# Where the output-gate fold, the quantum columns and half of the modulation loads stand in an adaLN retention layer

## The chip, the cores and the metric

The kernel runs on the 8 cores of one Trainium2 chip. Each core computes one element of the batch, with the whole layer on it; the cores exchange nothing. The metric is the device time in microseconds (us) of the slowest core.

## What is computed

For each of 8 batch elements (2048 rows of 1024), with a modulation vector from a small matrix product:

```python
mod = (silu(c) @ wmod).reshape(B, 6, 1, -1)            # c: 8 x 1024, wmod: 1024 x 6144
sa, ca, ga, sb, cb, gb = (mod[:, k] for k in range(6))
ga, gb = clamp away from zero: sign(g) * max(|g|, 0.25)
h = layernorm(x) * (1 + ca) + sa
x = x + ga * ((silu(h @ W_G) * groupnorm(retention(h @ Wq, h @ Wk, h @ Wv))) @ W_O)
h = layernorm(x) * (1 + cb) + sb
x = x + gb * (relu(quantum(h @ W1 + b1)) @ W2 + b2)
# quantum(z) = z + 0.1 * (cos(th) * wr + sin(th) * wi) * wi * sin(th + 0.1 * z), th, wr, wi: 4096 values
```

Retention has 8 heads of 128 columns and a causal decay of its own per head.

## The kernel before

The program has three blocks, each ended by a barrier of all engines: the prologue (`blk_p`), phase A with the retention (`blk_a`), and phase B with the feed-forward part (`blk_b`). Helpers of the class `Prog` record operations in program order, one list per engine; a block's list is issued by its engine strictly in that order, and waits on semaphores are put in where a tile was written or read by another engine. `dma_in` puts a load on SyncE's queue and lets four be in flight, `dma_cast` puts one on GpSimd's queue (two in flight; it may change the type), `dma_out` one on ScalarE's.

The prologue loads constants, makes `silu_cols` and four sets of 32 columns (`b1_cols`, `th_cols`, `wr_cols`, `wi_cols`), and calls `emit_matvec_half(0)` (L429 is its matmul). The matrix-vector product with `wmod` has two halves of 3072 output columns. For each of 8 blocks of rows `dk` and 4 parts it loads a piece of 128 x 768 f32 (384 KB) to one of two slots of `wmp` and does 6 matmuls of one column into bank 6 of PSUM; after the four parts VectorE adds the 24 columns to `macc` (L440). The third of the parts thus needs the slot of the first. After the call in program order come the casts of X tiles 0 and 1, of the four weights wq, wk, wv and wg (8 pieces each) and of X tiles 2 to 15: 48 in all, each read as 512 KB of f32 and landed as 256 KB of bf16 (L176 is the helper's line). Then `clamp_cols` and `cols_to_tile` make `ga_tile` from half 0; 16 multiplications (L532) fold `ga_tile` into W_O as `wo_bf`, each with a 256 KB load to one of two slots of `wstage`; and some 75 small operations of VectorE and four Sin of ScalarE (L540 to L588) make the quantum columns `p_cols` and `r_cols`, which are read first in phase B.

Phase A goes over 8 groups of 256 rows. Group g issues `stage_W(g-2)` (output projection with `wo_bf`, from L897), `stage_R(g-1)` (retention, from L738), `stage_Pmm(g)` (the four projections; `wg` ends it), `stage_Pstats(g+1)` (layer-norm statistics, its last operation writes `hpre`, L623) and, for g up to 5, one or two rows of blocks of `emit_matvec_half(1)`: `mod_pieces` gives row 0 to group 0 and rows 1 and 2 to group 1. Phase B keeps both large weights in memory that phase A's tiles had, so it loads them (L176, 64 casts) behind the barrier, and goes over 8 groups of rows again.

Of the kernel before, what the change touches and what calls it, by code (L numbers as in the profile page):

```python
# [255 lines left out]
def _emit(nc, usage, debug, upto="B"):  # L256
# [15 lines left out]
    wm_h = nc.dram_tensor("L0_wmod", [D, 6 * D], F32, kind="ExternalInput").ap()  # L272
# [5 lines left out]
    dbg_h = {}  # L278
# [11 lines left out]
    with ExitStack() as ctx:  # L290
        P = Prog(nc, ctx, usage)

        def alloc(c_, name, pdim, fdim, dtype=F32):
            return c_.enter_context(nc.sbuf_tensor(name, [pdim, fdim], dtype))
# [22 lines left out]
        ab_ctx = ctx.enter_context(ExitStack())  # L317
# [101 lines left out]
        def emit_matvec_half(half, dks=range(8)):  # L419
            for dk in dks:  # L420
                for part in range(4):
                    s = (dk * 4 + part) % 2
                    c0h = half * 3072 + part * 768
                    P.dma_in(wmp[:, s * 768:(s + 1) * 768],
                             wm_h[dk * 128:(dk + 1) * 128, c0h:c0h + 768],
                             writes=[("wmp", s)])
                    for c in range(6):
                        ci = part * 6 + c
                        P.op("tensor", lambda e, s=s, c=c, ci=ci, dk=dk: e.matmul(  # L429
                                psum[6][:, ci:ci + 1],  # L430
                                wmp[:, s * 768 + c * 128:s * 768 + (c + 1) * 128],
                                silu_cols[:, dk:dk + 1],
                                start=True, stop=True),
                             reads=[("wmp", s), "silu_cols"], writes=[("pb", 6)])
                mk = ("macc", half)
                if dk == 0:
                    t_copy("vector", macc[:, half * 24:half * 24 + 24],
                           psum[6][:, 0:24], [("pb", 6)], [mk])
                else:
                    P.op("vector", lambda e, half=half: e.tensor_add(  # L440
                            macc[:, half * 24:half * 24 + 24],
                            macc[:, half * 24:half * 24 + 24], psum[6][:, 0:24]),
                         reads=[("pb", 6), mk], writes=[mk])

        def emit_mod_right_final():
# [7 lines left out]
                 reads=["gb_cols", "b2_cols"], writes=["ctmp2"])  # L453
            cols_to_tile(ctmp2, "ctmp2", gbb2_tile, "gbb2_tile")

        with ExitStack() as pctx:
            cstage = alloc(pctx, "cstage", 8, 128)
            b2stage = alloc(pctx, "b2stage", 8, 128)
            vstage = alloc(pctx, "vstage", 32, 4 * 128)
            th_cols = alloc(pctx, "th_cols", 128, 32)  # L460
            wr_cols = alloc(pctx, "wr_cols", 128, 32)
            wi_cols = alloc(pctx, "wi_cols", 128, 32)
            beta_cols = alloc(pctx, "beta_cols", 128, 32)
            tmpc = alloc(pctx, "tmpc", 128, 32)
            tmpc2 = alloc(pctx, "tmpc2", 128, 32)
            sth_cols = alloc(pctx, "sth_cols", 128, 32)
            cth_cols = alloc(pctx, "cth_cols", 128, 32)
            a_cols = alloc(pctx, "a_cols", 128, 32)

            for name, dst in [("ones_row", ones_row), ("mask4_t", mask4_t),  # L470
                              ("id_bf", id_bf), ("id_f32", id_f32),
# [51 lines left out]
            clamp_cols(ga_cols, "ga_cols", 16)  # L523
            cols_to_tile(ga_cols, "ga_cols", ga_tile, "ga_tile")

            for dk in range(8):
                for hf in range(2):
                    stg = (dk * 2 + hf) % 2
                    P.dma_in(wstage[:, stg * 512:(stg + 1) * 512],
                             Wo_h[dk * 128:(dk + 1) * 128, hf * 512:(hf + 1) * 512],  # L530
                             writes=[("wstg", stg)])
                    P.op("vector", lambda e, dk=dk, stg=stg, hf=hf: e.tensor_mul(  # L532
                            wbf["wo"][:, dk * 1024 + hf * 512:dk * 1024 + (hf + 1) * 512],
                            wstage[:, stg * 512:(stg + 1) * 512],
                            ga_tile[:, hf * 512:(hf + 1) * 512]),
                         reads=[("wstg", stg), "ga_tile"], writes=[("wo", dk, hf)])

            def reduce_range(key, buf):
                for _ in range(8):
                    P.op("vector", lambda e: e.tensor_scalar(  # L540
# [50 lines left out]
            if debug:  # L591
                P.dma_out(dbg_h["d_pcols"], p_cols[:, :], reads=["p_cols"])
                P.dma_out(dbg_h["d_rcols"], r_cols[:, :], reads=["r_cols"])
                P.dma_out(dbg_h["d_ga"], ga_tile[:, :], reads=["ga_tile"])

            if upto == "P":
                P.final_join()
            with nc.Block("blk_p") as blk:
                P.flush(blk)
            if upto == "P":  # L600
                return P.usage

        with ExitStack() as actx:

# [332 lines left out]
            for g in range(NG):  # L937
                if g >= 2:
                    stage_W(g - 2)
                if g >= 1:  # L940
                    stage_R(g - 1)
                stage_Pmm(g)
                if g + 1 < NG:
                    stage_Pstats(g + 1)
                if g in mod_pieces:
                    emit_matvec_half(1, dks=mod_pieces[g])
            stage_W(NG - 2)
# [213 lines left out]
```

## Time and profile before

| | us |
|---|---|
| median of 2 runs | 2183.44 |
| lowest, highest | 2179.59, 2187.28 |
| device time of the profiled execution | 2194.06 |
| span of its slowest core (core 7), from first to last instruction | 2192.5 |
| spans of its eight cores | 2170.7 to 2192.5 |

The profile is one execution, on its slowest core. PE is TensorE's matmuls, PEld its weight loads, DVE VectorE, ACT ScalarE, POOL GpSimd, SP SyncE; a q behind an engine's name means its queue of DMAs and semaphores. L numbers are lines of the kernel before. PEclk is TensorE's granted clock, as a share of full speed. Times in the trace count from the span's start. The views that are read are the page's engine rows and slices, a table of busy time by stretch, lists of instructions in order of time (idle time before an instruction, and what ended it, stand in brackets), one line's instructions and the DMA answers of a stretch.

### The profile page before, as it was taken

The page shows a single profiled execution, that of the slowest core. Times are in us where ns is not written, and L with a number is a line of the kernel's source. Part 1 is how long each engine was busy: PE and PEld are TensorE (multiplying, and loading weights), DVE is VectorE, ACT ScalarE, POOL GpSimd, SP SyncE. Part 2 cuts the span into 40 slices and gives each one's busy share as a digit, 9 for nine tenths or more (in the row PEclk, how much of TensorE's full clock was granted, in tenths as well). Part 3 has the DMA queues.
Part 4 walks back from the last instruction along what each step waited for, and adds up shares of the span by engine and source line. Part 5 has one row for each costly group of instructions (what it writes and reads, how often), then busy time and mean ns, then how long its engine had stood idle before and what let it go on. Part 6 is the DMA issues. An engine that isn't in the chain of part 4 may idle for free.

```text
span 2192.5 us, 23636 instructions; the slowest of 8 cores (2170.7 to 2192.5 us)
## 1 busy us (share of the span) xinstructions
PE 1186.4 (54%) x6720; PEld 733.7 (33%) x6720; DVE 747.0 (34%) x1759; ACT 573.9 (26%) x1255; POOL 93.4 (4%) x132
## 2 busy tenths in 40 slices
PE   3553358484848575473503323474747474756564
PEld 3552236252534353241101111242424242423232
DVE  0002532434353434434301111434353435353433
ACT  0000032122122212222001111343434343434343
POOL 1110000000000000000011110000000000000000
PEclk9999967676867776776556666796969797979888
DMA  7882011010001010000143442000000000000000
GB/s 148 163 163 91 15 29 37 22 30 1 30 1 30 1 44 1 1 1 1 17 65 58 63 62 43 20 1 20 1 20 1 20 1 20 1 20 1 10 11 20
DMA packets 33616, 70.12 MB, mean 32 GB/s; under 512 B 4161, under 2 KB 4434, under 8 KB 33490
## 3 DMA queue, kind: packets, MB, share of 16 engines
q0 software_dynamic: 16128, 29.37, 9.3%
q1 hardware_dynamic: 12754, 30.85, 4.7%
q10 hardware_dynamic: 4608, 8.39, 1.0%
q8 instruction: 58, 0.95, 0.2%
q14 instruction: 68, 0.56, 0.1%
HBM read 89.56 MB, written 8.39 MB: 45 GB/s over the span
## 4 chain that ended last, share of the span: by engine, by line
DVE 15%; ACT 11%; DMA 11%; issue 9%; PE 2%; ACTq 1%; DVEq 1%; POOL 0%; POOLq 0%
DMA w2bf<-L_ffn_W 6%; ACT csin L1051 5%; DMA w1bf<-L_ffn_W 5%; DVE t1b L1065 5%; DVE t1b L1060 5%; ACT csin L1056 4%; DVE h2r L1016 1%; DVE outr L1110 1%; DVE outr L1105 1%; PE pb L1081 1%; PE pb L1010 1%; DVE stats L984 1%; ACT sqscr L989 1%; DVE outr L1115 1%; PE pb L1041 1%
## 5 line engine op out<-in xcount | busy, mean ns | idle before, releaser
L1081 PE MATMUL pb<-w2bf,actb 128*128 128x512 bf16 x1024 | 280.2, 398 | 370.5 <-ACT actb L1070 256.1
L1060 DVE SCALAR_TENSOR_TENSOR t1b<-csin,p_cols,pb 128x256 f32<-128x256 bf16 x256 | 123.0, 480 | 613.9 <-ACT csin L1056 613.9
L1041 PE MATMUL pb<-h2r,w1bf 128*128 128x256 bf16 x2048 | 290.6, 290 | 73.7 <-DMA w1bf<-L_ffn_W 68.5
L1041 PEld LDWEIGHTS pb<-h2r,w1bf 128*128 128x128 bf16 x2048 | 211.7, 104 | 166.2 <-issue 85.8
L1081 PEld LDWEIGHTS pb<-w2bf,actb 128*128 128x128 bf16 x1024 | 87.2, 100 | 504.1 <-issue 446.6
L1070 ACT ACTIVATE actb<-t1b,b_cols 128x256 bf16<-128x256 f32 x256 | 130.6, 510 | 339.5 <-DVE t1b L1065 339.5
L429 PE MATMUL pb<-silu_cols,wmp 128*128 128x1 f32 x768 | 152.4, 330 | 81.3 <-DMA wmp<-L_wmod 81.2
L1051 ACT ACTIVATE csin<-pb,sb_halfpi_col,sb_tenth_col 128x256 bf16<-128x256 f32 x256 | 141.0, 551 | 174.2 <-PE pb L1041 174.1
L429 PEld LDWEIGHTS pb<-silu_cols,wmp 128*128 128x128 f32 x768 | 151.3, 303 | 83.9 <-issue 83.0
L641 PE MATMUL pb<-sb_id_bf,hpre 128*128 128x128 bf16 x128 | 32.8, 269 | 225.8 <-DVE h1r L646 161.8
L1065 DVE SCALAR_TENSOR_TENSOR t1b<-csin,r_cols,t1b 128x256 f32<-128x256 bf16 x256 | 123.8, 483 | 27.4 <-DVE t1b L1060 0.9
L1056 ACT ACTIVATE csin<-pb,sb_tenth_col 128x256 bf16<-128x256 f32 x256 | 118.8, 464 | 0.0
L910 PE MATMUL pb<-wo_bf,gfm 128*128 128x512 bf16 x256 | 91.0, 534 | 9.9 <-DVE gfm L903 9.9
L641 PEld LDWEIGHTS pb<-sb_id_bf,hpre 128*128 128x128 bf16 x128 | 13.5, 108 | 245.9 <-issue 245.9
L814 ACT ACTIVATE Mbf<-Mst 128x128 bf16<-128x128 f32 x128 | 27.5, 297 | 253.0 <-DVE Mst L803 245.1
L1010 PE MATMUL pb<-sb_id_bf,h2pre 128*128 128x128 bf16 x128 | 31.4, 271 | 94.1 <-DVE h2pre L1002 69.3
L664 PE MATMUL pb<-h1r,wq_bf 128*128 128x256 bf16 x512 | 75.8, 323 | 5.9 <-DVE h1r L646 5.9
L700 ACT ACTIVATE vtr<-pb 128x512 bf16<-128x512 f32 x32 | 19.1, 598 | 205.4 <-PE pb L691 205.4
L878 POOL TENSOR_TENSOR gated<-retn,gtr 128x1024 bf16<-128x1024 bf16 x16 | 33.9, 2117 | 846.1 <-ACT retn L867 779.5
L664 PEld LDWEIGHTS pb<-h1r,wq_bf 128*128 128x128 bf16 x512 | 58.3, 115 | 22.6 <-issue 7.2
L867 ACT ACTIVATE retn<-pb,stats 128x128 bf16<-128x128 f32 x128 | 58.9, 460 | 22.3 <-DVE stats L860 11.5
L897 PE MATMUL pb<-sb_id_bf,gated 128*128 128x128 bf16 x128 | 28.5, 243 | 61.8 <-DVE gfm L903 31.4
(139 smaller groups left out, 1195.7 us busy)
## 6 DMA issues: line engine op xcount, KB each, us to landing
wmp<-L_wmod SPq DMA_DIRECT2D x64, 384.0 KB, 4.0
w1bf<-L_ffn_W POOLq DMA_DIRECT2D x32, 256.0 KB, 4.1
w2bf<-L_ffn_W POOLq DMA_DIRECT2D x32, 256.0 KB, 4.0
OUT<-outr ACTq DMA_DIRECT2D x32, 256.0 KB, 2.0
xbf<-L_attn_X POOLq DMA_DIRECT2D x16, 256.0 KB, 6.4
wstage<-L_attn_W_O SPq DMA_DIRECT2D x16, 256.0 KB, 2.6
wq_bf<-L_attn_Wq POOLq DMA_DIRECT2D x8, 256.0 KB, 6.9
wk_bf<-L_attn_Wk POOLq DMA_DIRECT2D x8, 256.0 KB, 6.2
```

Of the source, the lines that this page charges most:

```text
L429: P.op("tensor", lambda e, s=s, c=c, ci=ci, dk=dk: e.matmul(psum[6][:, ci:ci + 1], wmp[:, s * 768 + c * 128:s * 768 + (c + 1) * 128], silu ...
L664: r0=r0: e.matmul(psum[pb][:, r0:r0 + 256], wbf[wnm][:, dk * 1024 + h * 128: dk * 1024 + (h + 1) * 128], h1r[:, dk * 256:(dk + 1) * 256], ...
L867: P.op("scalar", lambda e, h=h, pb=pb: e.activation(retn[:, h * 128:(h + 1) * 128], psum[pb][:, (h % 4) * 128:(h % 4 + 1) * 128], AF.Identity,
L910: P.op("tensor", lambda e, dk=dk, pb=pb, half=half: e.matmul(psum[pb][:, 0:512], gfm[:, dk * 128:(dk + 1) * 128], wbf["wo"][:, dk * 1024 + ...
L1010: P.op("tensor", lambda e, dk=dk, pb=pb: e.matmul(psum[pb][:, 0:128], h2pre[:, dk * 128:(dk + 1) * 128], id_bf[:, :], start=True, stop=Tru ...
L1041: P.op("tensor", lambda e, fk=fk, dk=dk, pbh=pbh, sl=sl: e.matmul(psum[pbh][:, 0:256], w1bf[:, dk * 4096 + fk * 128:dk * 4096 + (fk + 1) * ...
L1051: P.op("scalar", lambda e, pbh=pbh, cs=cs: e.activation(csin[:, cs * 512:cs * 512 + 256], psum[pbh][:, 0:256], AF.Sin, bias=halfpi_col[:, ...
L1056: P.op("scalar", lambda e, pbh=pbh, cs=cs: e.activation(csin[:, cs * 512 + 256:cs * 512 + 512], psum[pbh][:, 0:256], AF.Sin, scale=tenth_c ...
L1060: P.op("vector", lambda e, pbh=pbh, cs=cs, fk=fk: e.scalar_tensor_tensor(t1b[:, cs * 256:(cs + 1) * 256], csin[:, cs * 512:cs * 512 + 256] ...
L1065: P.op("vector", lambda e, cs=cs, fk=fk: e.scalar_tensor_tensor(t1b[:, cs * 256:(cs + 1) * 256], csin[:, cs * 512 + 256:cs * 512 + 512], r ...
L1070: P.op("scalar", lambda e, cs=cs, fk=fk: e.activation(actb[:, (fk % 4) * 256:(fk % 4 + 1) * 256], t1b[:, cs * 256:(cs + 1) * 256], AF.Relu ...
L1081: e.matmul(psum[pb][:, 0:512], actb[:, (fk % 4) * 256 + tsub * 128: (fk % 4) * 256 + (tsub + 1) * 128], w2bf[:, fk * 1024 + half * 512: fk ...
```

## The change

Three things are moved, and nothing is added to or taken from the arithmetic.

1. In half 0 of the matrix-vector product, the pieces for slot 1 of `wmp` (16 of 32) are issued with `dma_cast`, on GpSimd's queue, with no change of type. In program order they stand ahead of the 48 casts of X and the weights.
2. The 16 multiplications with their 16 loads become `wo_premult(dks)`, called in phase A: rows 0 to 3 behind `stage_Pstats(1)` in group 0, rows 4 to 7 behind `stage_Pstats(2)` in group 1, each time ahead of the group's share of `emit_matvec_half(1)`.
3. The quantum columns become `quantum_precompute()`, called in group 1 behind `wo_premult(range(4, 8))`, also ahead of the matrix-vector share. Nine small tiles that it uses live in phase A's memory now.

The first reader of `wo_bf` is `stage_W(0)` in group 2.

```diff
--- before.py
+++ after.py
@@ -421,9 +421,14 @@
                 for part in range(4):
                     s = (dk * 4 + part) % 2
                     c0h = half * 3072 + part * 768
-                    P.dma_in(wmp[:, s * 768:(s + 1) * 768],
-                             wm_h[dk * 128:(dk + 1) * 128, c0h:c0h + 768],
-                             writes=[("wmp", s)])
+                    if half == 0 and s == 1:
+                        P.dma_cast(wmp[:, s * 768:(s + 1) * 768],
+                                   wm_h[dk * 128:(dk + 1) * 128, c0h:c0h + 768],
+                                   writes=[("wmp", s)])
+                    else:
+                        P.dma_in(wmp[:, s * 768:(s + 1) * 768],
+                                 wm_h[dk * 128:(dk + 1) * 128, c0h:c0h + 768],
+                                 writes=[("wmp", s)])
                     for c in range(6):
                         ci = part * 6 + c
                         P.op("tensor", lambda e, s=s, c=c, ci=ci, dk=dk: e.matmul(
@@ -453,19 +458,20 @@
                  reads=["gb_cols", "b2_cols"], writes=["ctmp2"])
             cols_to_tile(ctmp2, "ctmp2", gbb2_tile, "gbb2_tile")
 
+        th_cols = alloc(ab_ctx, "th_cols", 128, 32)
+        wr_cols = alloc(ab_ctx, "wr_cols", 128, 32)
+        wi_cols = alloc(ab_ctx, "wi_cols", 128, 32)
+        beta_cols = alloc(ab_ctx, "beta_cols", 128, 32)
+        tmpc = alloc(ab_ctx, "tmpc", 128, 32)
+        tmpc2 = alloc(ab_ctx, "tmpc2", 128, 32)
+        sth_cols = alloc(ab_ctx, "sth_cols", 128, 32)
+        cth_cols = alloc(ab_ctx, "cth_cols", 128, 32)
+        a_cols = alloc(ab_ctx, "a_cols", 128, 32)
+
         with ExitStack() as pctx:
             cstage = alloc(pctx, "cstage", 8, 128)
             b2stage = alloc(pctx, "b2stage", 8, 128)
             vstage = alloc(pctx, "vstage", 32, 4 * 128)
-            th_cols = alloc(pctx, "th_cols", 128, 32)
-            wr_cols = alloc(pctx, "wr_cols", 128, 32)
-            wi_cols = alloc(pctx, "wi_cols", 128, 32)
-            beta_cols = alloc(pctx, "beta_cols", 128, 32)
-            tmpc = alloc(pctx, "tmpc", 128, 32)
-            tmpc2 = alloc(pctx, "tmpc2", 128, 32)
-            sth_cols = alloc(pctx, "sth_cols", 128, 32)
-            cth_cols = alloc(pctx, "cth_cols", 128, 32)
-            a_cols = alloc(pctx, "a_cols", 128, 32)
 
             for name, dst in [("ones_row", ones_row), ("mask4_t", mask4_t),
                               ("id_bf", id_bf), ("id_f32", id_f32),
@@ -523,7 +529,18 @@
             clamp_cols(ga_cols, "ga_cols", 16)
             cols_to_tile(ga_cols, "ga_cols", ga_tile, "ga_tile")
 
-            for dk in range(8):
+            if debug:
+                P.dma_out(dbg_h["d_ga"], ga_tile[:, :], reads=["ga_tile"])
+
+            if upto == "P":
+                P.final_join()
+            with nc.Block("blk_p") as blk:
+                P.flush(blk)
+            if upto == "P":
+                return P.usage
+
+        def wo_premult(dks):
+            for dk in dks:
                 for hf in range(2):
                     stg = (dk * 2 + hf) % 2
                     P.dma_in(wstage[:, stg * 512:(stg + 1) * 512],
@@ -535,6 +552,7 @@
                             ga_tile[:, hf * 512:(hf + 1) * 512]),
                          reads=[("wstg", stg), "ga_tile"], writes=[("wo", dk, hf)])
 
+        def quantum_precompute():
             def reduce_range(key, buf):
                 for _ in range(8):
                     P.op("vector", lambda e: e.tensor_scalar(
@@ -591,14 +609,6 @@
             if debug:
                 P.dma_out(dbg_h["d_pcols"], p_cols[:, :], reads=["p_cols"])
                 P.dma_out(dbg_h["d_rcols"], r_cols[:, :], reads=["r_cols"])
-                P.dma_out(dbg_h["d_ga"], ga_tile[:, :], reads=["ga_tile"])
-
-            if upto == "P":
-                P.final_join()
-            with nc.Block("blk_p") as blk:
-                P.flush(blk)
-            if upto == "P":
-                return P.usage
 
         with ExitStack() as actx:
 
@@ -942,6 +952,11 @@
                 stage_Pmm(g)
                 if g + 1 < NG:
                     stage_Pstats(g + 1)
+                if g == 0:
+                    wo_premult(range(0, 4))
+                elif g == 1:
+                    wo_premult(range(4, 8))
+                    quantum_precompute()
                 if g in mod_pieces:
                     emit_matvec_half(1, dks=mod_pieces[g])
             stage_W(NG - 2)
```

## Rows read from the trace of the kernel before

**Rows 1.** The page: the span, and busy time by engine.

```profile
span 2192.5 us, 23636 instructions; the slowest of 8 cores (2170.7 to 2192.5 us)
...
PE 1186.4 (54%) x6720; PEld 733.7 (33%) x6720; DVE 747.0 (34%) x1759; ACT 573.9 (26%) x1255; POOL 93.4 (4%) x132
```

**Rows 2.** Busy time by stretch: stretch, length, five engines, PEclk, DMA share, GB/s.

```profile
20.00:160.00 140.00, 76.09 (x346) 75.08 (x346) 1.91 (x12) 1.24 (x2) 22.29 (x43) 1.00 0.82 160
...
189.00:217.00 28.00, 0.00 (x0) 0.00 (x0) 10.74 (x18) 0.00 (x0) 0.00 (x0) 1.00 0.41 131
217.00:239.40 22.40, 0.00 (x0) 0.00 (x0) 13.93 (x76) 0.92 (x4) 0.00 (x0) 1.00 0.00 0
...
366.90:389.00 22.10, 18.18 (x99) 18.02 (x97) 3.40 (x10) 4.27 (x7) 0.00 (x0) 0.61 0.44 125
```

**Rows 3.** DMA issues in order of time, SyncE and then GpSimd: start, length, count.

```profile
19.89 148.78 SPq L163 DMA_DIRECT2D wmp<-L_wmod  x32
...
1.56 1.20 POOL L176 DMA_DIRECT2D xbf<-L_attn_X  x2 [0.86 <-POOLq L251]
8.62 0.53 POOL L176 DMA_DIRECT2D wq_bf<-L_attn_Wq  x1 [5.86 <-DMA xbf<-L_attn_X]
...
156.49 0.53 POOL L176 DMA_DIRECT2D xbf<-L_attn_X  x1 [1.60 <-DMA xbf<-L_attn_X]
```

**Rows 4.** In order of time, the matvec of half 0: start, length, engine, idle before.

```profile
154.15 5.25 PE L429 MATMUL pb<-silu_cols,wmp 128*128 128x1 f32 x24 [4.13 <-DMA wmp<-L_wmod]
```

**Rows 5.** In order of time, the rest of the prologue, VectorE and the barrier behind it.

```profile
174.84 0.18 DVE L440 TENSOR_TENSOR macc<-macc,pb 128x24 f32<-128x24 f32 x1 [15.09 <-PE pb L429]
...
188.69 1.29 DVE L532 TENSOR_TENSOR wo_bf<-wstage,ga_tile 128x512 bf16<-128x512 f32 x2
...
196.43 0.69 DVE L532 TENSOR_TENSOR wo_bf<-wstage,ga_tile 128x512 bf16<-128x512 f32 x1 [2.08 <-DMA wstage<-L_attn_W_O]
...
216.09 0.69 DVE L532 TENSOR_TENSOR wo_bf<-wstage,ga_tile 128x512 bf16<-128x512 f32 x1 [1.27 <-DMA wstage<-L_attn_W_O]
216.70 0.19 DVE L566 SCALAR_TENSOR_TENSOR beta_cols<-b_cols,th_cols 128x32 f32<-128x32 f32 x1
...
239.58 1.22 DVE L609 TENSOR_REDUCE stats<-xbf 128x1 f32<-128x1024 bf16 x1 [0.38 <-PEq L598]
```

**Rows 6.** Instructions of L598, the end of the prologue block: count, ns, first and last start.

```profile
L598 POOLq EVENT_SEMAPHORE  x2: 17/17/17, 239.3 to 239.4; - x2
L598 POOLq DRAIN  x1: 8111/8111/8111, 156.5 to 156.5; - x1
```

**Rows 7.** Casts alone, phase B: queue total and landing in 1080:1350, then one issue.

```profile
q0 software_dynamic: 9120, 16.62, 42.2%
...
w1bf<-L_ffn_W POOLq DMA_DIRECT2D x32, 256.0 KB, 4.1
...
1084.46 0.53 POOL L176 DMA_DIRECT2D w1bf<-L_ffn_W  x1 [4.09 <-DMA w1bf<-L_ffn_W]
```

**Rows 8.** DMA issues in 250:1060, SyncE pieces of half 1 alone.

```profile
wmp<-L_wmod SPq DMA_DIRECT2D x30, 384.0 KB, 3.1
```

**Rows 9.** In order of time, the end of group 0.

```profile
287.40 2.75 PE L429 MATMUL pb<-silu_cols,wmp 128*128 128x1 f32 x24
...
295.23 1.00 DVE L623 TENSOR_SCALAR hpre<-xbf,stats 128x1024 bf16<-128x1024 bf16 x2
...
297.60 1.01 PE L738 MATMUL pb<-sb_id_bf,ktr 128*128 128x128 bf16 x8 [0.43 <-DVE macc L341]
```

**Rows 10.** In order of time, the end of group 1.

```profile
366.89 2.73 PE L429 MATMUL pb<-silu_cols,wmp 128*128 128x1 f32 x24
...
372.84 1.28 ACT L344 ACT_TABLE_LOAD   x1 [1.43 <-DVE stats L369]
...
374.71 1.00 DVE L623 TENSOR_SCALAR hpre<-xbf,stats 128x1024 bf16<-128x1024 bf16 x2
...
388.91 0.37 PE L897 MATMUL pb<-sb_id_bf,gated 128*128 128x128 bf16 x2
```

## What I expect, and why

> **What bounds the kernel now.** I read the page's engine rows first [rows 1]. No engine is busy all the time; the busiest, TensorE, is at 54%. The profiled execution's slowest core spans 2192.5 us and the device time of that execution is 2194.06 us, some 1.6 us around the span. So the answer lies in each stage. The table by stretch [rows 2] shows the first 240 us: up to 160 us the sixteen DMA engines are 0.82 busy while TensorE is a little over half busy; from 189 us DMA is at 0.41, then at 0.00, and only VectorE works.
>
> The DMA queues explain the first part [rows 3]. SyncE issues 14 constants and then, from 19.89 us, 32 `wmp` pieces (384 KB each), double-buffered: a piece is issued when the matmuls of the piece two back are done. Beside it GpSimd issues 48 casts (X and four weights), two in flight, from 1.56 to 156.49 us. In a steady pair [rows 4] TensorE waits 4.13 us for DMA and does 24 matmuls in 5.25 us, so two pieces take 9.38 us. The matvec ends at 174.84 us.
>
> Then a serial chain [rows 5]: clamp and `ga_tile` (from 174.84 us), 16 multiplications of `wo` (first at 188.69, last at 216.09 us), and the quantum columns from 216.70 to 239.20 us. The block's end holds all five engines: GpSimd's DRAIN starts at 156.5 and takes 8.1 us, and the event semaphores of all come at 239.3 to 239.4 us [rows 6]. So phase A starts at 239.58 us, when VectorE is done; GpSimd's branch ends at 164.6 us and is hidden by 75 us. This cover is what the change lives on.
>
> **The change, part by part.** *1. wo and quantum leave the prologue.* VectorE's branch would lose 188.7 to 239.4, some 51 us. That is a gain only down to the next branch: GpSimd's.
>
> *2. The casts are queued behind the matvec.* `emit_matvec_half(0)` stands ahead of the casts in program order, and GpSimd issues in order. Its slot-1 pieces each wait for matmuls, so no cast is issued until the 16th piece is. Before, 48 casts ran beside the matvec; now they run after it.
>
> When does the matvec end? The 14 constants have SyncE's queue to 19.89 us with casts beside them; with one piece beside them I take the first slot-0 piece at 14 us (bounds 10 and 20) and its matmuls at 18.5 us, against 27.89 before. A pair's period is now set by slot 1: 2.63 us of matmul (half of 5.25), then the issue and landing on GpSimd's queue. The trace has no plain piece on that queue. Nearest above: a 512 KB-read cast alone, 4.62 us from issue to issue [rows 7]; below: a SyncE piece alone, landing in 3.1 us [rows 8], which with 2.63 us of matmul and some 0.4 us of issue and semaphore makes a pair of 6.15 us. I take 4.4 us, nearer the cast, as the queue is the same: 2.63 + 4.4 = 7.0 us a pair (6.15 to 7.3). The matvec ends at 18.5 + 16 x 7.0 = 130.5 us, 44 us earlier than before, and with `ga_tile` (188.69 less 174.84 is 13.9 us) VectorE would be free at 144 us.
>
> But GpSimd issues its last piece a pair before the end, at 123.5 us, cast 0 right behind, and cast 1 when that piece has landed, at 127.8 us. The 46 that follow go at a spacing c. Bounds: the DMA engines' own work is 42.2% of 270 us over 63 casts (16.62 MB at 0.262 MB), 1.8 us each [rows 7]; beside the matvec the spacing was (156.49 - 8.62) / 45 = 3.3 us [rows 3]. One cast alone has a cycle of 4.62 us; two in flight share it, 2.31 us. I take c = 2.35 us, because 1.8 us of engine work fits into it. The last cast is issued at 127.8 + 46 x 2.35 = 235.9 us; the drain adds about 5 us (4.1 us landing [rows 7], 8.1 us with neighbours [rows 6]). Phase A starts at 241.2 us instead of 239.6: **+2 us**. The 51 us taken off VectorE buy nothing, since the casts come out at the same place. With c = 1.8 it is -24 us, with c = 3.3 it is +45 us.
>
> For one transfer on this queue the Trainium skill (DMA: Bandwidth & Descriptors, "Anatomy of one DMA") gives 2.0 us plus bytes over 436 GB/s: an estimate from it is 3.2 us for 512 KB, where the trace shows 4.1 us. By that page cast spacing would be nearer the lower bound and the whole sum some 30 us lower; the first rival below is that case.
>
> *3. Group 0 of phase A.* Offsets are from 239.6. Before [rows 9]: the two `wmp` pieces of half 1 were fetched at the block's start, TensorE did 24 matmuls from 287.40 and 24 more by 297.2, VectorE copied `macc`, and stage_R(0) started at 297.60 (offset 58.0). Now SyncE has 8 `wstage` loads first. Two go at once; the third waits for the first multiplication, which stands on VectorE behind stage_Pstats(1), whose last `hpre` ends at 296.23 (offset 56.6). The `wmp` pieces are behind all of them, and TensorE's matvec and stage_R(0) wait for those. Multiplications repeat every 1.79 us (11 intervals from 196.43 to 216.09 [rows 5]): eight end at 68.8, the eighth load is issued at about 66.2, the first piece lands 3.3 us later, at 69.6. Four pieces then take a pair's period and the second pair's matmuls, 6.15 + 5.25 = 11.4 us: 81.0, and 0.4 us for the copy. stage_R(0) starts at 81.4 instead of 58.0: **+23.4 us**. VectorE's own 8 multiplications hide in this, the loads do not.
>
> *4. Group 1.* Offsets are from 366.89, TensorE's first matvec instruction [rows 10]. Before, stage_W(0) followed the 8 pieces at 388.91 (22.0). Now VectorE ends `hpre` at 8.8, multiplications end at 21.0, `wmp` pieces start at 17.8 and land at 21.5, and the first row's matmuls end at 33. The next row writes the same PSUM bank and needs `macc` added; that addition stands on VectorE behind the quantum columns: 21.0 + 22.5 (216.70 to 239.20 [rows 5]) + 1.3 for one ACT_TABLE_LOAD, as the Sin now follows a Sqrt (1.28 us each in the rows [rows 10]), = 44.8. Then 6.15 + 5.25 us of matmuls: 56.5. stage_W(0) starts 34.5 us later; the next Sqrt loads its table again, 1.3 us: **+35.8 us**. Nothing overlaps: TensorE's queue holds all later stages behind these matmuls. If only the quantum columns were hidden this would be +14 us. Later groups and phase B have the same instructions and come out as before; whether TensorE's granted clock dips longer after its new idle I take as 0, since it is at 0.61 in that stretch already [rows 2].
>
> Sum: +1.6 + 23.4 + 35.8 = +60.8 us on the profiled execution's 2194.06, that is 2255 us. The runs' median is 2183.44, 0.5% below that execution; on it the sum gives 2244 us, and I predict in those terms.
>
> **The rivals.** *A. Fast casts (c 1.8 to 2.05).* For: the DMA engines need only 1.8 us per cast, and were 0.82 busy before. Against: two in flight must then hide all of the fixed part. At c = 1.8, total 2 - 25 + 59 = +36 us or less with quicker pieces (6.15 us a pair gives another -13): 2206 to 2230, here 2215 us. Within 2% in most of it. 0.19.
>
> *B. Slow casts (c 2.8 to 3.3).* For: 3.3 us is what this queue did measure. Against: DMA engines carried 32 pieces besides. At c = 3.1, +34: total +95, 2278 us. 0.14.
>
> *C. Not slower: the block's end does not hold TensorE for GpSimd.* Then stage_Pmm(0) needs only the casts up to the last of `wg`, the 34th, landed at 127.8 + 32 x 2.35 + 4 = 207 us; its last matmuls would end at about 220 instead of 287 us: -67 + 59 = -8 us, 2175 us. It decides if phase A's first instruction comes ahead of 181 us. Against: the semaphores of all engines at 239.3 to 239.4 us, GpSimd's DRAIN among them [rows 6]. The same sign would come if the moved loads cost nothing. 0.05.
>
> *D. The moved work costs much less than I think* (VectorE takes multiplications early, or groups 0 and 1 have slack that the trace hides): +60.8 less half of 59: +31 us, 2215 us. Against: the order of each queue is fixed in the program. 0.07.
>
> **How the numbers follow.** My forecast (c 2.05 to 2.8) gets 0.55; its own range is +47 to +82, 2230 to 2265 us. A 0.19, B 0.14, C 0.05, D 0.07. The predicted time is 2244 us. The range takes in A's and D's centres and most of B: 2212 to 2282 us. 2% of 2183 is 44 us, about what a measurement of this kernel tells from no change; so slower by over 2% is my case and B and a part of A and D: 0.74. Faster by over 2% needs phase A to start ahead of 137 us, before the casts can be landed: 0.03. Within 2%: 0.23.
>
> **What the profile after should show.** GpSimd's first cast at about 124 us and the last at 236 us; matvec pairs 7.0 us apart, ending at 130 us; VectorE idle from 144 us to 241 us; DMA share about 0.4 before 125 us and 0.75 after; a TensorE hole of some 20 us ahead of the first half-1 matvec, and stage_R(0) 81 us after the block's end; in group 1 a second hole of 12 us while VectorE runs the quantum columns, stage_W(0) 56 us after `wg` ends. Phase B's length unchanged. Wrong would be: a last cast well off 236 us (my c), a `wmp` piece landing before the `wstage` loads are through (my queue order), or stage_R(0) starting before them.

## The result, and the profile after

The changed kernel is slower: a median of 2265.51 us (2257.77 to 2282.13, 11 runs) against 2186.86 us (2179.59 to 2198.48, 10 runs), ratio 1.0365 with a 95% interval of 1.0339 to 1.0390. The forecast was 2244 us, 2212 to 2282. In some executions four cores show a lower granted clock and take longer (2282.13 and 2274.53 us are two such runs), so that a median over few runs and the ratio beside it can differ by up to 0.5%. The page of the profiled execution begins:

```profile
span 2263.1 us, 23640 instructions; the slowest of 8 cores (2248.3 to 2263.1 us)
...
PE 1189.5 (53%) x6720; PEld 737.5 (33%) x6720; DVE 746.6 (33%) x1759; ACT 576.4 (25%) x1257; POOL 102.0 (5%) x148
```

Beside [rows 1] the busy times of all engines are the same within 4 us, POOL apart: it issues 16 DMAs more. So nearly all of the added time is waiting, and the table by stage says where. The stages end with the semaphores of the block ends, read on each of the eight cores:

| | before, profiled | changed, profiled |
|---|---|---|
| prologue ends, eight cores | 221.2 to 239.4 us, median 227.7 | 244.7 to 251.1 us, median 248.7 |
| phase A takes, median | 839.4 us | 898.8 us |
| phase B takes, median | 1111.8 us | 1108.3 us |
| core 7 alone: prologue, A, B | 239.4, 839.2, 1113.9 | 250.3, 898.8, 1114.0 |

So the prologue became 21 us longer on the median core and phase A 59 us.

**The prologue.** GpSimd's DMA issues in order of time (start, length, what ended the wait in brackets), where [rows 3] has the first cast at 1.56 and the last at 156.49 us:

```profile
24.71 0.55 POOL L176 DMA_DIRECT2D wmp<-L_wmod  x1 [22.43 <-PE pb L434]
...
121.71 0.54 POOL L176 DMA_DIRECT2D wmp<-L_wmod  x1 [7.24 <-PE pb L434]
122.23 0.55 POOL L176 DMA_DIRECT2D xbf<-L_attn_X  x1
...
127.54 0.53 POOL L176 DMA_DIRECT2D wq_bf<-L_attn_Wq  x1 [0.69 <-DMA xbf<-L_attn_X]
...
242.95 0.53 POOL L176 DMA_DIRECT2D xbf<-L_attn_X  x1 [1.93 <-DMA xbf<-L_attn_X]
```

Behind the first of these rows each piece waits 6.2 to 7.2 us for TensorE (14 such waits), and the first cast stands behind the last piece, at 122.23 us. Then a cast goes every (242.95 - 127.54) / 45 = 2.56 us. The table by stretch (stretch, length, busy time of the five engines, granted clock, DMA share, GB/s), against [rows 2]:

```profile
20.00:122.00 102.00, 79.86 (x361) 78.51 (x360) 1.26 (x7) 0.00 (x0) 7.81 (x15) 1.00 0.40 112
145.00:240.00 95.00, 0.00 (x0) 0.00 (x0) 0.00 (x0) 0.00 (x0) 19.52 (x37) 1.00 0.76 102
```

The DMA engines were 0.82 busy up to 160 us before. Now they are 0.40 busy during the matvec and 0.76 behind it. The work was spread out, and the stretch became longer. The instructions of the block's end (ns each, then first and last start) show who is last, as in [rows 6]:

```profile
L537 POOLq EVENT_SEMAPHORE  x2: 17/17/17, 250.2 to 250.3; - x2
...
L537 DVEq DRAIN  x1: 683/683/683, 141.9 to 141.9; - x1
L537 POOLq DRAIN  x1: 7201/7201/7201, 242.9 to 242.9; - x1
```

VectorE is at the barrier at 142 us and GpSimd at 250.1; before it was 239.3 and 164.6. The branch that had 75 us of cover now has none.

The matvec itself became quicker: it ends at 128.6 us, and with its start at 18.85 us that is 109.8 / 16 = 6.86 us a pair, against 9.38 [rows 4]. The DMA answers for the matvec and for the casts alone (issues, KB, median us to landing):

```profile
wmp<-L_wmod SPq DMA_DIRECT2D x15, 384.0 KB, 3.5
wmp<-L_wmod POOLq DMA_DIRECT2D x14, 384.0 KB, 3.5
...
wv_bf<-L_attn_Wv POOLq DMA_DIRECT2D x8, 256.0 KB, 4.6
```

A piece lands in 3.5 us from either queue. So the quicker pair is not GpSimd's queue but the missing casts: in group 1 below, where SyncE issues both pieces of a pair and no cast runs, a pair takes 6.24 us (448.78 to 455.02). The Trainium skill (DMA: Bandwidth & Descriptors, "Issuing engines are not separate DMA queues") says the same: DMAs issued by different engines run on the same 16 DMA engines and interleave, which saves only issue time. On that rule the trace agrees.

**Group 0.** In order of time:

```profile
307.27 8.59 SPq L163 DMA_DIRECT2D wstage<-L_attn_W_O  x6
...
316.21 11.13 SPq L163 DMA_DIRECT2D wmp<-L_wmod  x4
...
321.67 5.25 PE L434 MATMUL pb<-silu_cols,wmp 128*128 128x1 f32 x24 [23.74 <-DMA wmp<-L_wmod]
...
334.17 1.01 PE L748 MATMUL pb<-sb_id_bf,ktr 128*128 128x128 bf16 x8 [0.44 <-DVE macc L341]
```

SyncE issues the third to eighth `wstage` load from 307.27 us, one per multiplication, and the pieces only at 316.21. TensorE waits 23.74 us for them, and stage_R(0) starts at 334.17, 83.9 us behind the block's end, where [rows 9] has 58.2.

**Group 1.** `wg` ends at 403.9 us:

```profile
422.77 37.92 SPq L163 DMA_DIRECT2D wmp<-L_wmod  x10
...
426.49 5.25 PE L434 MATMUL pb<-silu_cols,wmp 128*128 128x1 f32 x24 [22.62 <-DMA wmp<-L_wmod]
...
448.46 0.18 DVE L445 TENSOR_TENSOR macc<-macc,pb 128x24 f32<-128x24 f32 x1
...
448.78 5.25 PE L434 MATMUL pb<-silu_cols,wmp 128*128 128x1 f32 x24 [10.80 <-DVE macc L445]
455.02 5.25 PE L434 MATMUL pb<-silu_cols,wmp 128*128 128x1 f32 x24 [0.99 <-DMA wmp<-L_wmod]
...
460.14 0.37 PE L907 MATMUL pb<-sb_id_bf,gated 128*128 128x128 bf16 x2
```

TensorE waits 22.62 us for the pieces behind the loads, then 10.80 us for the `macc` addition, which VectorE does at 448.46, right behind the last quantum operation. stage_W(0) starts 56.3 us behind `wg`, against 22.0 in [rows 10].

### The profile page after: what moved, and what is told of

It reads as the page before. It is cut to its first block, busy times and chain, and to the rows that moved or that the text cites. A ratio compares the mean times of both kernels' runs of the same rounds, so it can differ in the third digit from the quotient of the medians.

```text
span 2263.1 us, 23640 instructions; the slowest of 8 cores (2248.3 to 2263.1 us)
## 1 busy us (share of the span) xinstructions
PE 1189.5 (53%) x6720; PEld 737.5 (33%) x6720; DVE 746.6 (33%) x1759; ACT 576.4 (25%) x1257; POOL 102.0 (5%) x148
## 4 chain that ended last, share of the span: by engine, by line
DVE 15%; ACT 11%; DMA 11%; issue 9%; PE 2%; ACTq 1%; DVEq 1%; POOL 0%; POOLq 0%
DMA w2bf<-L_ffn_W 5%; ACT csin L1066 5%; DMA w1bf<-L_ffn_W 5%; DVE t1b L1080 5%; DVE t1b L1075 5%; ACT csin L1071 4%; DVE h2r L1031 1%; DVE outr L1125 1%; DVE outr L1120 1%; DVE stats L999 1%; ACT sqscr L1004 1%; PE pb L1025 1%; DVE outr L1130 1%; PE pb L1096 1%; ACTq L83 1%
## 5 line engine op out<-in xcount | busy, mean ns | idle before, releaser
L1096 PE MATMUL pb<-w2bf,actb 128*128 128x512 bf16 x1024 | 281.2, 399 | 371.6 <-ACT actb L1085 255.4
L434 PE MATMUL pb<-silu_cols,wmp 128*128 128x1 f32 x768 | 157.9, 336 | 95.6 <-DMA wmp<-L_wmod 81.3
L434 PEld LDWEIGHTS pb<-silu_cols,wmp 128*128 128x128 f32 x768 | 156.1, 310 | 99.1 <-issue 98.5
L619 DVE TENSOR_REDUCE stats<-xbf 128x1 f32<-128x1024 bf16 x16 | 19.4, 1215 | 206.9 <-PEq L537 108.0
L674 PEld LDWEIGHTS pb<-h1r,wq_bf 128*128 128x128 bf16 x512 | 58.1, 114 | 22.4 <-issue 7.2
```

The lines of the kernel that those rows point to most:

```text
L434: P.op("tensor", lambda e, s=s, c=c, ci=ci, dk=dk: e.matmul(psum[6][:, ci:ci + 1], wmp[:, s * 768 + c * 128:s * 768 + (c + 1) * 128], silu ...
L674: r0=r0: e.matmul(psum[pb][:, r0:r0 + 256], wbf[wnm][:, dk * 1024 + h * 128: dk * 1024 + (h + 1) * 128], h1r[:, dk * 256:(dk + 1) * 256], ...
L1096: e.matmul(psum[pb][:, 0:512], actb[:, (fk % 4) * 256 + tsub * 128: (fk % 4) * 256 + (tsub + 1) * 128], w2bf[:, fk * 1024 + half * 512: fk ...
```

## The experiments

Two theories of the prologue stood against each other. By the **queue theory** the block ends when GpSimd's in-order queue is through, and it is late because its casts stand behind pieces that wait for TensorE. By the **work theory** the shared DMA engines need that long for all transfers, in whatever order. For phase A the question was whether the delay comes from the order in the queues or from VectorE's added work as such. "Changed" in what follows is the kernel of the forecast. Ratios are to the kernel before, with 95% intervals.

**1. All pieces on SyncE again (`sync_slots`).**

```diff
-                    if half == 0 and s == 1:
-                        P.dma_cast(wmp[:, s * 768:(s + 1) * 768], ...
-                    else:
-                        P.dma_in(...)
+                    P.dma_in(wmp[:, s * 768:(s + 1) * 768], ...
```

> The changed kernel with one part undone: all 32 pieces of the matrix-vector half 0 are issued by SyncE again; wo and the quantum columns stay in phase A. Queue theory (GpSimd's casts, queued behind its own pieces, end the prologue): the casts run beside the matvec again, the prologue ends with ga_tile at about 175 to 189 us (before: 221 to 239 on the eight cores, changed: 245 to 251), some 50 us earlier than before; phase A keeps its 59 us more; total +9 us on before, ratio 1.004, 69 us faster than the changed kernel. Rival (DMA work theory: the prologue is as long as all its transfers take on the shared DMA engines, whichever queue issues them): the prologue still ends at about 245 us and the ratio stays at 1.036.

Measured: 1.0032 (1.0015 to 1.0050), 2191.57 us. The prologue ends at 166.9 to 181.1 us, median 177.8; phase A takes 898.8 us, phase B 1109.7. The block's end on its slowest core, core 0:

```profile
L532 POOLq EVENT_SEMAPHORE  x2: 17/17/17, 177.7 to 177.8; - x2
...
L532 POOLq DRAIN  x1: 8269/8269/8269, 153.7 to 153.7; - x1
...
L532 DVEq DRAIN  x1: 683/683/683, 177.0 to 177.0; - x1
```

GpSimd is through at 162.0 and VectorE at 177.7 us. The work theory is out: the same transfers are done 88 us earlier. One of the three parts costs 71 us on the median core, and without it the rest is worth +7 us: 50 us out of the prologue, 59 into phase A and 2 less in phase B.

**2. The pieces alone (`gpsimd_slots_only`).**

```diff
@@ the kernel before
+                    if half == 0 and s == 1:
+                        P.dma_cast(wmp[:, s * 768:(s + 1) * 768], ...
```

> The kernel before with the first part alone: slot 1 of the matrix-vector half 0 issued by GpSimd ahead of the casts; wo and quantum columns stay in the prologue. Queue theory: matvec ends at 129 us, VectorE's branch at 129 + 14 + 51 = 194 us, but the last cast goes at about 240 and the block ends at 245 to 251 us, 21 us later than before on the median core and 11 us on the slowest; phases A and B as before; ratio 1.005 to 1.010. DMA work theory: the same work in the same time, ratio 1.000. Faster matvec theory (the casts are hidden whatever their place): the block ends at 194 us, ratio 0.98.

Measured: 1.0121 (1.0081 to 1.0162), 2211.48 us; prologue 251.2 to 262.0, median 255.4 us; phase A 837.3. The sign is that of the queue theory; the size is above its range of 1.005 to 1.010, though the interval reaches into it. The block's end and two stretches:

```profile
L603 POOLq EVENT_SEMAPHORE  x2: 17/17/17, 256.5 to 256.5; - x2
...
L603 DVEq DRAIN  x1: 189/189/189, 208.4 to 208.4; - x1
L603 POOLq DRAIN  x1: 7226/7226/7226, 249.2 to 249.2; - x1
...
145.00:195.00 50.00, 0.00 (x0) 0.00 (x0) 15.44 (x46) 0.00 (x0) 8.97 (x17) 1.00 0.90 165
195.00:250.00 55.00, 0.00 (x0) 0.00 (x0) 8.40 (x46) 0.92 (x4) 11.61 (x22) 1.00 0.72 103
```

VectorE's whole branch is done at 208.6 and waits 48 us for GpSimd's DRAIN. The 7 us beyond the changed kernel's 248.7: SyncE issues the `wstage` loads up to 181.4 us here, among the casts (share 0.90), and in the changed kernel they are not in this stretch. While they run, the casts go 2.87 us apart (127.73 to 182.31 us, 19 steps), and behind them 2.57 (182.31 to 249.20, 26 steps); 19 x 0.30 is 6 of the 7 us. No run took the loads out alone.

**3. The quantum columns alone (`quantum_only`).**

```diff
@@ the kernel before; wo_premult(range(8)) stays in the prologue
+                if g == 1:
+                    quantum_precompute()
                 if g in mod_pieces:
                     emit_matvec_half(1, dks=mod_pieces[g])
```

> The kernel before with the quantum columns alone moved to group 1, behind the statistics and ahead of the matrix-vector share; all pieces on SyncE, wo in the prologue. Order theory: the prologue ends 22.5 us earlier (199 to 217 us); in group 1 the macc addition waits for the columns, to 8.8 + 22.5 + 1.3 = 32.6 us behind wg, then 11.7 us of matmuls, stage_W(0) at 44.4 instead of 22.0, and one table load more: +23.7 us; net +1 us, ratio 1.000 to 1.001. Rival (VectorE is idle two thirds of phase A and takes the columns in for nothing): ratio 0.990.

Measured: 0.9956 (0.9932 to 0.9980), 2176.30 us. Prologue 204.2 us (median), phase A 854.5 us, 15 us more than before, where 24 were expected. TensorE in group 1:

```profile
333.62 2.73 PE L429 MATMUL pb<-silu_cols,wmp 128*128 128x1 f32 x24
338.59 5.25 PE L429 MATMUL pb<-silu_cols,wmp 128*128 128x1 f32 x24 [2.24 <-DMA wmp<-L_wmod]
365.81 5.25 PE L429 MATMUL pb<-silu_cols,wmp 128*128 128x1 f32 x24 [21.97 <-DVE macc L440]
...
377.37 0.37 PE L903 MATMUL pb<-sb_id_bf,gated 128*128 128x128 bf16 x2
```

TensorE waits 21.97 us for the `macc` addition, and stage_W(0) starts 43.75 us behind its first matvec instruction instead of 22.0. With the table load, group 1 is 24.4 us longer on this core (from the first gating multiplication of one group to that of the next, 134.2 against 109.8 us) and 22.4 on the median core (133.9 against 111.5). This step was right. But the three groups behind it are 3.2, 0.9 and 2.7 us shorter on this core; see the last section. The rival of 0.990 is out; the 1.000 of the order theory lies above the interval too, by what those groups give back.

**4. Work behind the share (`share_first`).** As in 1, with the order within a group turned round:

```diff
-                if g == 0: wo_premult(range(0, 4)) ...
                 if g in mod_pieces:
                     emit_matvec_half(1, dks=mod_pieces[g])
+                if g == 0: wo_premult(range(0, 4)) ...
```

> All pieces on SyncE; in groups 0 and 1 the matrix-vector share stands ahead of the moved wo multiplications and quantum columns, in every queue. Order theory (the delay passes to whichever queue stands ahead of stage_R and stage_W): SyncE's loads no longer hold the pieces, so TensorE's share is done at 58 us of the block as before the change, but VectorE then runs 8 multiplications before the copies of stage_R(0), +12 us, and 8 multiplications and the quantum columns before those of stage_W(0), +37 us; phase A 49 us longer than before against 59 with the loads ahead; with the prologue 50 us shorter the ratio is 0.999 to 1.000. Rival (the delay is SyncE's queue alone): phase A as before, ratio 0.977.

Measured: 0.9971 (0.9943 to 1.0000), 2182.09 us; phase A 884.4 us, 45 more than before. Groups 0 and 1 in order of time:

```profile
234.39 0.18 DVE L341 COPY macc<-pb 128x24 f32<-128x24 f32 x1 [2.61 <-PE pb L429]
...
247.94 1.28 DVE L751 CAST ktm<-pb 128x512 bf16<-128x512 f32 x2
...
248.77 1.18 PE L757 MATMUL pb<-qtr,ktr 128*128 128x128 bf16 x8 [13.03 <-DVE ktm L751]
...
340.28 0.37 PE L902 MATMUL pb<-sb_id_bf,gated 128*128 128x128 bf16 x2
...
340.70 1.29 DVE L544 TENSOR_TENSOR wo_bf<-wstage,ga_tile 128x512 bf16<-128x512 f32 x2
...
377.60 0.68 DVE L908 CAST gfm<-pb 128x128 bf16<-128x128 f32 x2
```

The share is done in time (`macc` at 234.39 us), and then VectorE multiplies until 248.0 while the copies of stage_R(0) wait, 12.6 us. In group 1 stage_W(0)'s transposes start at 340.28 us, but their copy `gfm` comes at 377.60, 37 us later. The rival, SyncE's queue alone, is out. The delay moved from SyncE's queue to VectorE's: it belongs to the place in the order, and no queue is free at that place.

**5. Four casts in flight (`four_casts`).** In the changed kernel:

```diff
-            for j in range(2):
+            for j in range(4):
                 self.sems[f"gdma{j}"] = ...
-            sem_name = f"gdma{j % 2}"
+            sem_name = f"gdma{j % 4}"
```

> The changed kernel with four transfers in flight on GpSimd's queue instead of two. In the changed kernel the casts alone go 2.56 us apart (127.54 to 242.95 us in 45 steps) at a DMA share of 0.76, which is 1.93 us of DMA engine work each. Latency theory (two in flight leave the engines idle between casts): the spacing falls to 1.9 to 2.0 us, the last cast goes at about 215 us, the block ends near 222 us instead of 245 to 251, total 27 us faster than the changed kernel, ratio 1.024. Rival (GpSimd's own descriptor work or the memory sets 2.56 us): spacing, block end and ratio 1.036 stay.

Measured: 1.0123 (1.0068 to 1.0179), 2219.73 us; the block ends at 202.2 to 208.7 us, median 206.3. The issues and a stretch, core 2:

```profile
128.45 0.53 POOL L176 DMA_DIRECT2D wq_bf<-L_attn_Wq  x1 [0.85 <-DMA xbf<-L_attn_X]
...
201.24 0.53 POOL L176 DMA_DIRECT2D xbf<-L_attn_X  x1 [1.46 <-DMA xbf<-L_attn_X]
...
140.00:205.00 65.00, 2.04 (x2) 0.49 (x2) 0.69 (x1) 0.00 (x0) 19.61 (x37) 1.00 1.06 159
```

The spacing is (201.24 - 128.45) / 43 = 1.69 us at a share of 1.06 (the share can pass 1; why, the trace doesn't show). So in the 2.56 us the engines waited for landings with two in flight. Latency theory right, its size too small: the block ends 42 us earlier than in the changed kernel instead of 27, as 1.93 us of share time per cast was not a floor. The median time is 46 us shorter than the changed kernel's.

**6. A version that beats both (`placed`).** All pieces on SyncE. Each multiplication of `wo`, with its load, stands behind one evacuation of q or k; the quantum columns stand in phase B:

```diff
@@ stage_Pmm(g), behind the tensor_mul that evacuates q or k
+                            if g < 2:
+                                wo_one(g * 8 + (0 if scaled else 4) + quad * 2 + bi)
@@ phase B
                     ln2_stats(0)
                     ln2_tr(0)
+                    quantum_precompute()
```

> A version meant to beat both: all pieces on SyncE; each of the 16 wo multiplications stands behind one evacuation of q or k in stage_Pmm(0) and stage_Pmm(1), where VectorE waits 1.05 us for TensorE each time; the quantum columns stand in phase B behind the first layer norm, where all engines wait for the feed-forward weights. Order theory: the prologue gives 50 us, phase A and phase B cost 0 to 5 us; ratio 0.977 to 0.980. Rival (moved VectorE work costs its length wherever it stands): 11 us of multiplications and 24 us of columns come on top, ratio 0.993.

Measured: 0.9762 (0.9727 to 0.9797), 2133.45 us; prologue 173.1 us, phase A 836.6, phase B 1107.2. Both covers hold: phases A and B are even 3 and 5 us shorter than before, which no row here explains. VectorE in stage_Pmm(0), and TensorE at the start of phase B, core 3:

```profile
208.73 0.69 DVE L681 TENSOR_TENSOR ktr<-pb,sb_kscale_t 128x512 bf16<-128x512 f32 x1 [0.29 <-PE pb L668]
209.34 0.68 DVE L543 TENSOR_TENSOR wo_bf<-wstage,ga_tile 128x512 bf16<-128x512 f32 x1
210.47 0.69 DVE L681 TENSOR_TENSOR ktr<-pb,sb_kscale_t 128x512 bf16<-128x512 f32 x1 [0.46 <-PE pb L668]
...
1061.93 3.57 PE L1048 MATMUL pb<-h2r,w1bf 128*128 128x256 bf16 x16 [21.88 <-DVE sth_cols L588]
1094.65 1.86 PE L1088 MATMUL pb<-w2bf,actb 128*128 128x512 bf16 x4 [29.16 <-DMA w2bf<-L_ffn_W]
```

These evacuations stay 1.74 us apart with a multiplication between them (1.75 without, read from the kernel before). From the first to the last of the eight it is 13.85 us against 13.46 before; in the last gap a multiplication waits 0.93 us for its load. In phase B TensorE waits 21.88 us and 29.16 us for `w2bf`. The first row names VectorE, but in the kernel before the same wait is there, 20.91 us, and ends with the DMA of `w1bf`; here the eighth cast of `w1bf` goes at 1056.60 and takes some 4.6 us to land, so the weight comes at about the same time. The columns end at 1063.70, 1.8 us after TensorE has begun and long before `w2bf` is there.

**7. Four pieces in flight (`placed_4slots`), and four casts too (`placed_4slots_4casts`).** Half 0 borrows two tiles that the prologue does not use:

```diff
-                    s = (dk * 4 + part) % 2
+                    s = part if half == 0 else part % 2
+                    buf, o = [(wmp, 0), (wmp, 768), (Mst, 0), (sqscr, 0)][s]
```

> The placed version, and in half 0 four slots for the pieces (two borrowed tiles that the prologue does not use). Latency theory: TensorE waits 4.13 of 9.38 us a pair for a landing; with four pieces in flight the DMA engines become the limit: 48 x 1.8 + 32 x 1.3 + 4.5 = 133 us of work at a share of 0.95 is 140 us, the block ends at about 155 us on all cores instead of 169 to 180; 20 us faster than the placed version, ratio 0.967. Rival (the engines already deliver what they can at a share of 0.85, more in flight only lands later): the block's end stays at 169 to 180 us, ratio 0.976.

> The same with four casts in flight as well. If the DMA engines are the limit with four pieces in flight, four casts take share from the pieces: casts end some 15 us earlier, the pieces land later, the matvec ends 5 to 15 us later, ratio 0.969 to 0.975. If latency is still the limit, both end earlier: ratio 0.962 or less.

Measured: 0.9674 (0.9584 to 0.9765), 2123.26 us, and 0.9594 (0.9531 to 0.9658), 2100.79 us; median over median these are 0.9720 and 0.9617, and the two intervals overlap. The prologue, where the two differ, ends at 160.6 and at 144.1 us (medians). The stretch 20 to 130 us of core 0 in `placed`, `placed_4slots` and `placed_4slots_4casts`:

```profile
20.00:130.00 110.00, 68.56 (x306) 67.04 (x306) 1.73 (x11) 0.00 (x0) 18.20 (x35) 1.00 0.88 175
```

```profile
20.00:130.00 110.00, 92.80 (x412) 87.10 (x412) 5.67 (x25) 0.00 (x0) 16.91 (x32) 1.00 0.90 192
```

```profile
20.00:130.00 110.00, 86.95 (x394) 85.68 (x394) 1.97 (x13) 1.46 (x2) 20.61 (x39) 1.00 1.04 213
```

The share goes from 0.88 over 0.90 to 1.04, 175 to 213 GB/s. Four pieces gave 12.5 us of the 20 expected. Of the two outcomes written for the last, the one with latency still the limit came out: a share of 0.82 to 0.90 is not a full one.

**8. The same rule in phase B (`phase_b_4casts`, `phase_b_split`).** Phase B's casts wrote under one key for eight, so each waited for the one before it. Now each has its own, the matmuls wait for the one piece that they read, and four are in flight as in the prologue:

```diff
-                               writes=[("w1g", qt)], chain=(dk == 0), sem_idx=0,
-                               force_inc=True)
+                               writes=[("w1g", qt, dk)])
```

> The version with placed work, four slots and four casts in flight, and the same rule in phase B: each of its 64 casts has its own key and four are in flight, where before one at a time was (4.62 us from issue to issue). Flight theory: the spacing falls to the 1.65 us that four in flight gave in the prologue, the weights are in after 64 x 1.65 = 106 us instead of 272, and the first of phase B's eight groups (1079 to 1398 us before) takes about as long as the others (115 us) plus its start and the layer norm: phase B 150 to 180 us shorter, ratio 0.88 to 0.89. Rival (the memory or GpSimd sets the pace in phase B): ratio 0.959 as without it. The quantum columns, 24 us at the start of phase B, lose part of their cover.

> The same, with the range reduction of the quantum columns in two parts of 9.6 us in phase A, each between stage_Pmm and stage_Pstats of groups 2 and 3, where VectorE waits 13.7 us for ScalarE's square; 3.5 us of Sin and products stay in phase B. Cover theory: phase A unchanged, and phase B's first activation comes up to 19 us earlier, 10 to 20 us faster than the run beside it (ratio 0.870 to 0.885). Rival (the columns were still hidden in phase B, as the first weights take as long): no difference.

Measured: 0.8817 (0.8709 to 0.8925), 1936.55 us, and 0.8803 (0.8734 to 0.8873), 1932.76 us; median over median 0.8855 and 0.8838. Phase B takes 945.8 us instead of 1111.8. Spacing in `phase_b_4casts`: (1099.92 - 990.21) / 63 = 1.74 us, against 4.62 for one cast at a time [rows 7], so the last of the 64 is issued some 63 x 2.88 = 181 us earlier. What the finer keys give beside this was not run by itself. Splitting the quantum columns takes 5 us off phase B (940.9 us), where 10 to 20 were expected, and nothing that the two ratios tell apart. A stretch of `phase_b_split`, the time of the casts:

```profile
985.00:1098.00 113.00, 64.91 (x336) 34.60 (x337) 37.31 (x91) 42.20 (x91) 33.32 (x63) 0.79 1.01 144
```

The DMA engines are full until the last weight is in. The first matmul that reads `w2bf` comes 24.7 us into the block with the columns split and 44.4 us without (core 7 and core 5, the slowest of each run), as the expectation had it. But TensorE then waits for weights, 3.81 us for `w1bf` ahead of 1062.09 us for one, and the 20 us shrink to 5.

## Why the prediction was right, and by how much not

The forecast went by core 7 of the profile before. Step by step, for that core:

| step | forecast | measured |
|---|---|---|
| matvec: first matmul, pair, end | 18.5, 7.0, 130.5 us | 18.85, 6.86, 128.6 us |
| first cast issued | 123.5 us | 122.2 us |
| spacing of the casts alone | 2.35 us | 2.56 us |
| last cast, phase A's start | 235.9, 241.2 us | 242.95, 250.3 us |
| stage_R(0) late by | 23.4 us | 25.7 us |
| stage_W(0) late by | 34.5 us | 34.3 us |
| phase A, both and the table load | +59.2 us | +59.6 us |
| sum on core 7 | +60.8 us | +70.6 us |

The mechanism was right at every step. The casts take the place of VectorE as the last branch (runs 1 and 2 show it by itself), the quantum columns hold the `macc` addition (run 3), and the moved loads hold SyncE's queue. The loads had no run of their own. For them stand the rows of group 0, where nothing else is moved, and run 4, in which they come behind the share and TensorE's hole ahead of it is gone. Rival C, a block end that does not hold TensorE, fell: all engines' semaphores come when GpSimd's DRAIN is done. Rival D, moved work at half its price, fell with the 59.6 us of phase A. Rival A fell too: at two in flight the casts were not fast. Rival B's 2.8 us was not reached.

The forecast was 21.5 us short of the median, and three things make this up. **The prologue's terms** are 9 us of it. For the spacing c I halved the cycle of a cast that runs alone, 4.62 us, so that two in flight would cost each other nothing. They do: landing takes 4.6 us instead of 4.1, and with 0.53 us of issue half the cycle is 2.56 us, or 46 x 0.21 = 10 us more. Of these the start took 2.6 back: the third cast goes at 127.54 us, where the forecast has it at 127.8 + 2.35. The drain took 7.2 us instead of 5. **The profiled execution** was 7.2 us above the median of the runs before (2194.06 against 2186.86), and the one after 0.9 below (2264.61 against 2265.51), so 70.6 us on core 7 are 79 us between the medians. In that execution core 7 was slowest because its prologue was late, 239.4 us where the median of the cores was 227.7. The changed prologue ends within 6.4 us on all cores, and the median core lost 21 us in it where core 7 lost 11. The ends of one stage on all cores would have shown beforehand that core 7 is no measure for this stage. **The base** of two runs, 2183.44 us, was 3.4 us below the median of ten.

Phase A agrees to 0.4 us, and that is in part luck: the two holes came out 2.3 longer and 0.2 shorter, and 1.7 us were given back elsewhere in the phase.

Three side figures of the forecast do not hold. The lower bound of c, 1.8 us, was 6% too high as a bound: it came from the DMA share of casts that run alone, and run 5 went to 1.69 at a share of 1.06. In group 1, with the quantum columns hidden and the `macc` addition right behind the first row's matmuls at 33, my own terms give stage_W(0) 34.5 - (44.8 - 33) = 23 us late, not 14; the rows agree, with 10.80 of the 34.3 us spent on that addition. And the page of the Trainium skill that I weighed (DMA: Bandwidth & Descriptors, "Anatomy of one DMA", 3.2 us for 512 KB by its fit) gives less than was measured, 4.1 us alone and 4.6 us for two in flight, with eight cores loading. By that fit half a cycle would be (3.2 + 0.53) / 2 = 1.87 us, an estimate, and the sum 22 us lower, not some 30. None of the three entered the sum.

## What to carry to other kernels

Before a load is moved to another queue or work behind another stage, list what stands behind it there on every engine that it touches: a load that waits for an engine holds every load behind it, and work taken off one branch of a barrier gains only down to the next branch, whose end has to be read on every core. Moved work is free only where its own engine waits anyway (behind an evacuation, beside a long load) and where its loads stand ahead of no one else's; "later in the same group" was 49 to 58 us dearer than that here (runs 4 and 1 against run 6). Where loads set the pace and the DMA share is no more than the 0.4 to 0.9 seen here, first put more of them in flight: that took 42 us off the changed prologue and, with finer waits, 166 us off phase B.

## What was not expected of the hardware

Groups with the same instructions differ by 3 us with the granted clock. From the first gating multiplication of one group to that of the next, in the kernel before, in `quantum_only` (core 7 of each) and on core 0 of `placed`:

```profile
432.10:530.60 98.50, 64.10 (x384) 40.35 (x384) 39.45 (x102) 23.23 (x53) 4.26 (x3) 0.73 0.06 17
```

```profile
423.50:518.90 95.40, 61.12 (x384) 39.96 (x384) 39.51 (x102) 23.23 (x53) 4.26 (x3) 0.77 0.06 17
```

```profile
367.10:463.20 96.10, 62.05 (x384) 39.59 (x384) 39.48 (x102) 23.27 (x53) 4.27 (x3) 0.75 0.06 17
```

The counts are equal on all engines and VectorE's busy time is too. TensorE is busy 61.12 instead of 64.10 us at a mean granted clock of 0.77 instead of 0.73, between the two levels of 1.2 and 2.4 GHz. In `quantum_only` this group follows one in which TensorE had waited 22 us, and it takes 95.2 to 95.6 us on seven of the eight cores and 98.2 on one, where the kernel before has 98.3 to 98.9 on all eight. In the changed kernel, behind longer holes, it takes 97.0 to 97.5 us, at 0.75 on core 7. So a part of the hole's cost seems to come back behind it, some 7 us in `quantum_only` (24.4 more in group 1, but 16 at the end of phase A on core 7) and 2 us in the changed kernel (25.7, 34.3 and 1.3 against 59.6).

The hole is not the only thing that does this. `placed` has no such hole, and its cores 0, 1 and 7 take 95.9 to 96.0 us for this group while the others take 98.5 to 99.0; in the kernel before, cores 3 and 5 take 96.0 and 96.1 us for the group after it. What decides between the two lengths stays open: no run changed a hole alone.
